# A transformer and state-space layer in 16 passes: quantiser with one step less, 1/sigma applied at the residual, rms norm folded into its layer norm, stacking waited for by groups

## The reference, cut to what matters

```python
def _layernorm(x, eps=1e-5):            # rows of 256, no gain and no bias
    return (x - mean(x)) / sqrt(var(x) + eps)
x = x + attention(_layernorm(x))        # 16 heads of 16, rotary, causal softmax
x = x + ffn(_layernorm(x))              # quantised product, below
y = _layernorm(x)                       # the third one feeds the block
z = y + mamba_mixer(rmsnorm(y))         # rmsnorm: t * rsqrt(mean(t*t) + 1.1920929e-7)
z = z + silu(rmsnorm(z) @ w1.T) @ w2.T
x = x + z
x = x + ffn(_layernorm(x))
# ffn(t): in blocks of 32 columns, scale = max(|t|)/7.5, t/scale rounded to the nearest of
# a grid of 6-bit floats (ties to the lower one), times scale; the same for the weight;
# then xd @ wd.T + bias
```

## Time and profile before

| | us |
|---|---|
| three runs before: median (lowest, highest) | 10044.25 (10041.67, 10044.95) |
| the profiled execution, its own time | 10042.81 |
| span of its instructions | 10040.9 |
| granted TensorE clock, mean (of 1.00) | 0.898 |
| VectorE busy | 7696.5 |
| TensorE matmul busy | 7867.1 |

### The profile page before, as it was taken

The page is one execution under the profiler, slowest core; times in us unless marked ns, Lnnn a source line. Parts: engine busy times, 40 slices in busy tenths (PEclk is TensorE's granted clock), DMA queues, the critical chain, the costliest instruction groups (busy, mean ns, idle before and its releaser), DMA issues. The chain is left out here.

```text
span 10040.9 us, 98208 instructions
## 1 busy us (share of the span) xinstructions
PE 7867.1 (78%) x31796; PEld 3819.5 (38%) x31796; DVE 7696.5 (77%) x11686; ACT 4309.5 (43%) x8247; POOL 4340.3 (43%) x2663
## 2 busy tenths in 40 slices
PE   5787787787877878787887878778787787877877
PEld 2343343433434334343343433434343343432434
DVE  4787877779687686876868768787787877878777
ACT  2534535354442543525435254353534535345352
POOL 1451714518154171542716336262361724517145
PEclk8898988989889898888989889898898988989889
DMA  3010020200202002020020200102011020100202
GB/s 76 1 38 15 5 48 1 51 1 5 48 0 51 1 9 44 0 51 1 12 40 0 51 1 21 32 0 52 1 28 25 0 52 1 38 15 5 48 0 51
DMA packets 260295, 229.91 MB, mean 23 GB/s; under 512 B 22051, under 2 KB 232739, under 8 KB 259635
## 3 DMA queue, kind: packets, MB, share of 16 engines
q1 hardware_dynamic: 259782, 223.48, 11.6%
HBM read 151.60 MB, written 70.25 MB: 22 GB/s over the span
## 5 line engine op out<-in xcount | busy, mean ns | idle before, releaser
L625 POOL TENSOR_TENSOR arena<-arena 128x1024 f32<-128x1024 f32 x1024 | 2434.3, 2387 | 1330.6 <-DVE arena L1007 879.0
L766 ACT ACTIVATE PS<-arena,Aneg 128x512 f32<-128x512 f32 x2048 | 1410.6, 691 | 1627.2 <-DVE XNT L1047 883.2
L690 ACT ACTIVATE arena<-PS 128x512 f32<-128x512 f32 (+3 forms) x3072 | 1286.8, 509 | 867.0 <-PE PS L1213 861.8
L914 DVE TENSOR_REDUCE pm<-PS 128x1 f32<-128x512 f32 (+3 forms) x1728 | 1050.6, 661 | 336.5 <-PE PS L1192 234.9
L1327 PE MATMUL PS<-XNT,identf 128*128 128x512 f32 x2048 | 1012.1, 618 | 320.0 <-POOL XNT L608 320.0
L587 POOL TENSOR_SCALAR_AFFINE_SELECT arena<-arena 128x512 f32<-128x512 f32 x512 | 328.2, 641 | 2114.5 <-ACT arena L690 2114.5
L1189 PE MATMUL PS<-arena 96*128 96x512 bf16 (+3 forms) x3072 | 1098.0, 382 | 178.8 <-PEq L1411 87.3
L1327 PE MATMUL PS<-arena,identf 128*128 128x512 f32 x2048 | 1025.5, 624 | 161.8 <-DVE arena L1023 161.8
L1213 PE MATMUL PS<-arena 99*128 99x512 bf16 (+3 forms) x3072 | 891.8, 331 | 5.4
L1150 PE MATMUL PS<-identf,arena 128*128 128x128 f32 x1280 | 284.1, 387 | 776.0 <-POOL arena L577 664.6
L1312 PE MATMUL PS<-arena,sel 96*128 96x512 bf16 x1664 | 513.4, 391 | 389.2 <-DVE arena L1023 319.7
(11 more groups left out here) (140 smaller groups left out, 13240.7 us busy)
## 6 DMA issues: line engine op xcount, KB each, us to landing
pieces_scratch<-arena SPq DMA_DIRECT2D x816, 64.0 KB
arena<-pieces_scratch SPq DMA_DIRECT2D x34, 768.0 KB
arena<-pieces_scratch SPq DMA_DIRECT2D x51, 512.0 KB
arena<-pieces_scratch SPq DMA_DIRECT2D x17, 1536.0 KB
arena<-in_x SPq DMA_DIRECT2D x17, 1024.0 KB, 5.6
U<-in_x SPq DMA_DIRECT2D x17, 1024.0 KB, 5.6
arena<-pieces_scratch SPq DMA_DIRECT2D x17, 1024.0 KB
out<-X SPq DMA_DIRECT2D x64, 256.0 KB, 8.3
```

The costliest lines, as they stand in the source:

```text
L625: nc.gpsimd.tensor_tensor(DB[:, n % 2], DTU[:, j, half(th)].unsqueeze(1).to_broadcast([P, SP2, TH]), BB[:, SP2 * sg:SP2 * (sg + 1), :], AL ...
L690: A(PT[s % len(PT)][:, hh, 0:w], bank(t_bank(n))[:, 0:w], ACT.Exp, scale=DH ** -0.5)\
L766: A(bank(da_bank(m)), DT[:, j, half(th)], ACT.Exp, scale=Aneg[:, j, SP2 * sg + ss:SP2 * sg + ss + 1]).then_inc(S("dA"), 1)
L914: V_.tensor_reduce(out=dst, in_=bank(r % 3)[:, 0:share * w].rearrange("p (h w) -> p h w", h=share), op=ALU.max, axis=AX.X, negate=True).th ...
```

## The change

- The quantiser computes the upper candidate and the lower one as before, then takes the minimum while both still carry the large constant (with the upper one multiplied by 1 - 2^-24, so that it is one step lower), and removes the constant once. Ten operations instead of eleven.
- The rows that are quantised are only centred (`centre`, one operation with the mean), without waiting for 1/sigma; 1/sigma multiplies the product at the residual (`add_scaled`).
- 1/rms of the normalised rows is computed from the variance directly (`vr`, `joint_power`), and the normalised and rms-normalised rows are made from `X` in one operation (`joint_rows`), ahead of the layer norm that writes `U`. ScalarE's squares for this norm are gone.
- The second half of K and the whole of Q are stacked by groups of four heads, 24 transfers instead of 6, each group with a semaphore of its own. TensorE waits for a group's semaphore before its first scores. SyncE no longer waits for them at the end of a pass; it waits for them and clears them later, after the last maxima are written.

```diff
             step(... out=src, in0=h, scalar=ROUND + 2, in1=v, op0=ALU.mult, op1=ALU.add))
             step(lambda scl, rcp, amx, v, h, a, src: STT(
-                out=a, in0=h, scalar=-ROUND, in1=a, op0=ALU.mult, op1=ALU.add))
-            step(lambda scl, rcp, amx, v, h, a, src: STT(
-                out=src, in0=h, scalar=-ROUND - 2, in1=src, op0=ALU.mult, op1=ALU.add))
+                out=a, in0=src, scalar=ONE_STEP_DOWN, in1=a, op0=ALU.mult, op1=ALU.min))
             for n, (scl, rcp, amx, v, h, a, src) in enumerate(lanes):
                 own.wait(at[n])
-                yield TT(v, a, src, ALU.min)
+                yield STT(out=v, in0=h, scalar=-ROUND, in1=a, op0=ALU.mult, op1=ALU.add)
...
-        N_STACK = 1 + 3 * len(RUNS[0])
+        N_STACK = 1 + len(RUNS[1])
+        N_GROUP = 16 * (len(RUNS[0]) + len(RUNS[1]))
...
             sp.wait_ge(S("pcd"), N_PCD * NT // 2)
-            stack(sp, 1, ALL, half(1))
-            if in_loop:
-                sp.wait_ge(S("pj"), NT * 3)
-            stack(sp, 0, ALL, slice(0, T))
+            for g in range(NG):
+                heads = slice(g * HG, (g + 1) * HG)
+                stack(sp, 1, heads, half(1), stacked[g])
+                if in_loop and g == 0:
+                    sp.wait_ge(S("pj"), NT * 3)
+                stack(sp, 0, heads, slice(0, T), stacked[g])
...
+            for g in range(NG):
+                sp.wait_ge(stacked[g], N_GROUP)
+                sp.sem_clear(stacked[g])
             sp.wait_ge(S("dB"), NM)
...
+            def joint_power(th):
+                pool.wait_ge(S("var"), NTH + th + 1)
+                nc.gpsimd.tensor_tensor(rms[:, tiles(th)], vr[:, tiles(th)], mhalf[:, tiles(th)], ALU.pow)\
+                  .then_inc(S("rm"), 1)
...
             quantized(0, 0, 1)
+            joint_power(0)
             layer_power(1, 0)
+            joint_power(1)
             layer_power(1, 1)
-            rms_power(0, 0)
-            rms_power(0, 1)
...
             evacuate(1)
-            squares(0, "xn", NT)
             evacuate(2)
...
+            if joint:
+                V_.tensor_scalar(vr[:, which], mv[:, which, 1], 1.0 + RMS_EPS, RMS_EPS * LN_EPS, ALU.mult, ALU.add)
...
+            def centre(th, dst):
+                for i in range(NT)[tiles(th)]:
+                    V_.tensor_scalar(dst(i), X[:, i, :], mv[:, i, 0:1], None, ALU.subtract).then_inc(S("xn"), 1)
...
+            def add_scaled(stage, i):
+                if i % (NT // NTH) == 0:
+                    dve.wait_ge(S("rstd"), NTH * (stage - 1) + i * NTH // NT + 1)
+                dve.wait_ge(S("pj"), NT * stage + i + 1)
+                V_.scalar_tensor_tensor(out=X[:, i, :], in0=bank(row_bank(stage, i))[:, 0:C], scalar=rstd[:, i:i + 1],
+                                        in1=X[:, i, :], op0=ALU.mult, op1=ALU.add).then_inc(S("x1"), 1)
...
-                layer_norm(k, th, lambda i: quant_rows(f, i // 2)[:, i % 2, :])
+                centre(th, lambda i: quant_rows(f, i // 2)[:, i % 2, :])
...
+            def joint_rows(th):
+                dve.wait_ge(S("rm"), th + 1)
+                for i in range(NT)[tiles(th)]:
+                    V_.tensor_scalar(RM[0][i], X[:, i, :], mv[:, i, 0:1], rms[:, i:i + 1],
+                                     ALU.subtract, ALU.mult).then_inc(S("R"), 1)
...
-            add_tiles(1, X)
+            add_tiles(1, lambda i: add_scaled(1, i))
+            for th in range(NTH):
+                joint_rows(th)
             for th in range(NTH):
                 layer_norm(1, th, lambda i: U[:, i, :])
-            for th in range(NTH):
-                rms_rows(0, th)
...
             for i in range(NT):
-                add_tile(3, X, i)
+                add_scaled(3, i)
...
+                    if u % NS1 == 0:
+                        pe.wait_ge(stacked[g], N_GROUP)
```

More of the change, by code:

```diff
@@ L36 @@
 ROUND = 1.5 * 2.0 ** 24
+ONE_STEP_DOWN = 1.0 - 2.0 ** -24
 TWO_ONES = 1.0 + 127 / 2.0 ** 16
@@ L123, in build @@
         ve = sb("ve", [P, NT])
+        vr = sb("vr", [P, NT])
         rstd = sb("rstd", [P, NT])
@@ L192, in build @@
         RM[1][0:NT // NTH] = [view(31248 + C * i, C) for i in range(NT // NTH)]
-        SQ = [view(at, 2048).rearrange("p (i c) -> p i c", i=NT) for at in (26640, 14336)]
+        SQ = view(14336, 2048).rearrange("p (i c) -> p i c", i=NT)
         TZ, TM = (view(at, 1024).rearrange("p (n t) -> p n t", n=2) for at in (28688, 13312))
@@ L333, in build @@
         landed = ctx.enter_context(nc.semaphore("out_landed"))
+        stacked = [ctx.enter_context(nc.semaphore(f"stacked_{g}")) for g in range(NG)]
         sem = {n: ctx.enter_context(nc.semaphore(n)) for n in names}
@@ L474, in build, with stack @@
         N_PCD = 16 * NC * 2 * PIECES
-        def stack(sp, qk, heads, cols):
+        def stack(sp, qk, heads, cols, done):
             row = 0
@@ L482, in stack @@
                              pcd[qk, heads, lo:hi, :, cols].rearrange("h n d t -> (n d) h t"))\
-                  .then_inc(S("stack"), 16)
+                  .then_inc(done, 16)
                 row += n
@@ L501, in front_transfers @@
             ones_rows(sp, ALL)
-            stack(sp, 1, ALL, half(0))
+            stack(sp, 1, ALL, half(0), S("stack"))
             store_pieces(sp, 2)
@@ L632, in pool_program @@
             pad_v(own)
-            rms_power(1, 0)
+            rms_power(0)
             front_power(pool)
-            rms_power(1, 1)
+            rms_power(1)
             pool.wait_ge(S("R"), 2 * NT)
@@ L673, in evacuate, with squares @@
                       ACT.Copy).then_inc(S("te_done"), 1)
-            def squares(k, after, count, which=range(NT)):
+            def squares(which):
                 for i in which:
-                    act.wait_ge(S(after), count + i + 1)
-                    A(SQ[k][:, i, :], U[:, i, :], ACT.Square, accum_out=ms[:, i:i + 1]).then_inc(S("ms"), 1)
+                    act.wait_ge(S("u1"), i + 1)
+                    A(SQ[:, i, :], U[:, i, :], ACT.Square, accum_out=ms[:, i:i + 1]).then_inc(S("ms"), 1)
             for j in range(ND):
@@ L782, in scalar_program @@
             act.wait_ge(S("h"), NSC)
-            squares(1, "u1", 0, range(NT)[tiles(0)])
+            squares(range(NT)[tiles(0)])
             evacuate(3, range(NT // 4))
-            squares(1, "u1", 0, range(NT)[tiles(1)])
+            squares(range(NT)[tiles(1)])
             for n in range(NMLP):
@@ L802, in stats, with variance @@
             own.did(V_.bn_stats(st6[:, i, :], src[:, i, :]))
-        def variance(own, which, ready):
+        def variance(own, which, ready, joint=False):
             own.wait()
@@ L875, in tile_stats, with add_tiles @@
                 if i % (NT // NTH) == NT // NTH - 1:
-                    variance(own, tiles(i * NTH // NT), "var")
-            def add_tiles(stage, base):
+                    variance(own, tiles(i * NTH // NT), "var", stage == 1)
+            def add_tiles(stage, add):
                 for i in range(NT):
-                    add_tile(stage, base, i)
+                    add(i)
                     if i:
@@ L893, in quant_half, with rms_rows @@
             def quant_half(f, k, th):
-                layer_norm(k, th, lambda i: quant_rows(f, i // 2)[:, i % 2, :])
+                centre(th, lambda i: quant_rows(f, i // 2)[:, i % 2, :])
                 dve.wait_ge(S("xn"), NT * k + NT // NTH * (th + 1))
                 grid(f, range(th * NT // 4, (th + 1) * NT // 4))
-            def rms_rows(k, th):
-                dve.wait_ge(S("rm"), NTH * k + th + 1)
+            def joint_rows(th):
+                dve.wait_ge(S("rm"), th + 1)
                 for i in range(NT)[tiles(th)]:
-                    V_.tensor_scalar(RM[k][i], U[:, i, :], rms[:, i:i + 1], None, ALU.mult).then_inc(S("R"), 1)
+                    V_.tensor_scalar(RM[0][i], X[:, i, :], mv[:, i, 0:1], rms[:, i:i + 1],
+                                     ALU.subtract, ALU.mult).then_inc(S("R"), 1)
+            def rms_rows(th):
+                dve.wait_ge(S("rm"), NTH + th + 1)
+                for i in range(NT)[tiles(th)]:
+                    V_.tensor_scalar(RM[1][i], U[:, i, :], rms[:, i:i + 1], None, ALU.mult).then_inc(S("R"), 1)
             for u in range(U_END):
@@ L941, in vector_program @@
             dve.wait_ge(S("x_free"), 1)
-            add_tiles(0, U)
+            add_tiles(0, lambda i: add_tile(0, U, i))
             quant_half(0, 0, 0)
@@ L1059, in vector_program @@
             gate(NJT - 1)
-            rms_rows(1, 0)
+            rms_rows(0)
             dve.wait_ge(S("xf_loaded"), 16)
@@ L1074, in vector_program @@
                     if n == NORM_AT:
-                        rms_rows(1, 1)
+                        rms_rows(1)
                     if n == NORM_AT + 1:
@@ L1088, in vector_program @@
                 if n == NMLP - 4:
-                    layer_norm(2, 0, lambda i: quant_rows(1, i // 2)[:, i % 2, :])
+                    centre(0, lambda i: quant_rows(1, i // 2)[:, i % 2, :])
```

4 lines of the change are left out of this document (2 added, 2 removed).

## The result

The changed kernel takes 9802.05 us, median of 4 runs (9801.04 to 9804.51), beside 10044.21 us (10041.67 to 10044.95) for the kernel before: a ratio of 0.976, 95% interval 0.9748 to 0.9773. The forecast was 9797. The profiled execution took 9804.51 us, its span 9802.8.

What follows compares the result with a forecast made beforehand. No engine is near full (TensorE 78%, VectorE 77%), so stages were priced singly: 7.16 us in 16 passes, 7.45 in 15, 19.9 once, together 246 off 10042.8, giving 9797 us; 8-in-10 range 9767 to 9870.

Steps and rivals of the forecast that it cites:

- The quantiser's step: Quantiser in stages 1 and 3: one operation fewer saves 2.41 us a pass in stage 1, 2.65 in stage 3.
- two chains side by side: Up to the pass boundary: stacking transfers run beside the quantiser with its product, which is only 2.7 us shorter.
- Centring: Rows before quantising: fewer scalars give 0.7 us a pass, half in each stage; the ended wait for GpSimd's power 1.74, stage 3.
- the first half of stage 3: Centring there no longer waits for GpSimd's power: 0.5 us a pass taken, bounds 0 to 0.87.
- The scalar operand: Centring has one per-row scalar fewer on 16 rows a pass: 0.35 us net in each stage.
- The folded norm: From stage 1's statistics to the convolution: rms rows come earlier, 3.5 us plus 0.9 from TensorE's clock, 4.4 (3.3 to 5.4).
- Stacking by groups: Pass boundary: SyncE's stacking wait of 2.71 us a pass goes (1.2 to 3.2); before the loop 19.9 us once.
- bytes and packet length are unchanged: Stacking as 24 transfers: same data moved; at worst 18 more transfers at 0.6 us add 11 us to the chain.
- The cover for group 1: Start of a pass: group 1's stacking is complete 17 us before TensorE needs it, 7 in the worse case.
- The boundary stays: Rival: results issue only when stacking has drained, hiding all of stage 3's gain; 9909 us, chance 0.08.
- Slower: Rival: small transfers run at a much lower rate and hold SyncE up; 10200 us at a 54 us chain, chance 0.03.
- Small terms don't come: Rival: no clock gain, none from fewer scalars, only 1.24 us of the waits; 9831 us, chance 0.14.

## Why the forecast held, and where its reasons did not

**The quantiser's step** was priced right: 2.41 and 2.65 us forecast, 2.41 and 2.51 measured by putting the step back. It showed in full only because the boundary let it: alone, stage 3's 2.65 were lost, half to the stacking and half to TensorE's clock, which the forecast didn't have. The "two chains side by side" of the first part are borne out most plainly by the old stacking in the changed kernel, where the wait took all that stage 3 gained.

**Centring.** Forecast 2.44 us a pass, measured 3.03 (0.36 and 2.67). The step that failed in size is the first half of stage 3, taken at 0.5 within bounds of 0 and 0.87. The wait as a whole is worth 2.45 instead of 1.74, so that half gave 2.45 - 1.24 = 1.21. That is outside its bounds. The bound was set by how far GpSimd's bias sum can move forward; VectorE was also held up by GpSimd's operation before it, and now has its rows done as that one begins. The scalar operand was priced at 0.35 a stage; in stage 3 it gave 0.22.

**The folded norm.** 4.4 forecast, 3.97 measured; the chain's 3.5 came as described (from the first row behind the statistics to the first turn it is 925.92 - 925.14 = 0.78 us, before 966.81 - 962.41 = 4.40), and of the clock's 0.9 the rest, about half. The time at the low clock in this segment fell from 6.83 to 3.41 us, no further, as the clock fell 1.1 us into the turns. The run with `U` first shows that the order carries the gain, and that the work removed gives none without it: with that order the idle time is 6.46 us and the low clock is back at 6.83 us.

**Stacking by groups.** 2.71 us forecast, 2.93 measured (2.53 of it before the first score, 0.40 TensorE's clock behind it), for a reason that is wrong. The step that failed is "bytes and packet length are unchanged", from which I took the transfers to last as long as before or up to 11 us longer. They last 7 us less. With the wait kept, 9807 us, nearly all of the gain stays. The number came out all the same because the boundary is then set by `X`, whatever has freed it: it takes 3.87 us with the stacking alone, where the transfers end well before the last sum, and 3.92 in the changed kernel. What the missing wait would give with transfers as long as before was not run by itself. What is late next was named rightly: the last tile of `X`. The cover for group 1 was never tested, as no wait of TensorE on a group shows in the profile. SyncE issued 24 transfers in 11.79 us, less than the 13.7 forecast, and before the loop in 12.78.

**What the forecast didn't have** are +0.92 us in the sums of stage 3 and +0.38 in the scores. The quantiser ends 5.3 us earlier, and TensorE then stays at the low clock for 4.8 us behind the start of the last turns instead of 3.0; with the clock held high by extra products the sums take 6.20 us instead of 8.09. That the clock is the cause in the sums fits three values of the same kind, 7.17 us at 4.03 low, 8.09 at 5.88 and 8.55 at 6.81 (shorter quantiser alone): of each us more at the low clock half shows. The nine other kernels without extra products lie within 0.03 us of that line. It doesn't reach down to no low time at all, where it would give 5.15 and not 6.20 us: part of the low time lies ahead of the turns, where TensorE is idle, and at the high clock the turns wait for GpSimd (0.35 us). For the scores the case is weaker: they take 143.24 us with 25.5 us low, 143.69 with 25.8 (old stacking), 144.70 with 29.6 and 145.08 with 33.5, which goes the same way but not by one rate. Why the low stretch lasts longer when the quantiser ends earlier, no run shows by itself.

**The rivals.** "The boundary stays" (9909) is refuted by the first result, issued at 727.71, some 7 us before the stacking has drained (709.00 + 26.0 = 735.0), and by a boundary of 3.92 us. "Slower" asked for a longer chain of transfers; it went the other way. "Small terms don't come" (9831) falls with the centring's 3.03 us. That 9797 lies so near 9802 is in part luck, since the errors cancelled: a pass gained 0.6 us more than forecast by the centring and 0.2 at the boundary, and 0.4 less by the fold, 0.9 and 0.4 less by the sums of stage 3 and the scores. With 15 passes short by 0.93 us, 5.0 us more in the last pass (12.2 instead of 7.16, since stage 3 shortens that one too) and 0.9 more before the loop, the sum came out 8 us below 246.

## What to carry to other kernels

Where two chains run side by side up to a barrier, price an edit on one only up to the other's end, and try the edits together: the quantiser's step was worth 48 us alone, 39 of them in stage 1, and 83 with the stacking changed. Before you credit a wait's removal, run the kernel with the wait kept and look whether what it waits for has become shorter. When a stage on VectorE keeps TensorE idle, look at the granted clock of the products behind it; a few products that nobody reads, sized to end before the turns are due, took 1% off this kernel; with five and two more of them in the two gaps the gain was gone.

## What the runs showed of the hardware that was not expected

- The 2048-byte packets of one read-back take 251 ns in 6 large transfers, 188 in 24 small ones in the same order, and 165 to 167 with two targets in turn; 18 transfers more cost the queue 3.7 to 5.2 us of issuing (8.13 and 7.54 us for 6, 11.79 and 12.78 for 24) and the chain nothing.
- VectorE's four centring operations beside GpSimd's power on 128x4 took 1.49 us instead of 1.29, but 2.48 beside its operation on 128x512, and a product on 128x512 took 2.50 instead of 0.69 beside the sum on 128x1024.
- A change that only takes VectorE's work away lengthened TensorE's: the time at the low clock in the sums of stage 3 rose from 4.0 to 5.9 us, and 0.9 us of it showed. With the shorter quantiser alone it rose to 6.8 and took 1.38 of the 2.65 us that VectorE had given.
- Right behind the barrier of a pass the first maximum followed TensorE's first score after 1.07 us where the granted clock was 0.50, and after 0.67 us where it was at the high level: 0.40 us of the 2.93 that the boundary gave.
